# Cross attention: max scores in 13 chunks of 494 keys, one at every step behind the value products of that step; value products four slots further behind

## The reference, cut to what matters

```python
q = x @ Wq; k = ctx @ Wk; v = ctx @ Wv            # ctx: 6404 x 128
s = einsum('qd,kd->qk', q_h, k_h) / sqrt(8)       # 1024 x 6404 scores per head
p = softmax(s, axis=-1)                           # needs the max of each row
o_h = p @ v_h                                     # 1024 x 8
```

## Time and profile before

| | us |
|---|---|
| median of 3 runs (4591.18 to 4597.89) | 4594.65 |
| the profiled execution's own time | 4605.47 |
| its span | 4603.5 |
| PE busy | 3836.9 (83%) |
| DVE busy | 3455.6 (75%) |
| ACT busy | 2867.1 (62%) |
| mean granted TensorE clock, of full speed | 0.878 |

### The profile page before, as it was taken

One profiled execution on the slowest core, in us unless ns is written; L12 is line 12 of the kernel. 1 busy time (PEld: TensorE's weight loads), 2 busy tenths in 40 slices (PEclk: granted clock), 3 DMA queues, 4 the chain that ended last, 5 costly groups with the idle time before them and its releaser, 6 DMA issues. The chain is left out here.

```text
span 4603.5 us, 83947 instructions
## 1 busy us (share of the span) xinstructions
PE 3836.9 (83%) x34296; PEld 1292.0 (28%) x34358; DVE 3455.6 (75%) x3306; ACT 2867.1 (62%) x4073; POOL 258.4 (6%) x183
## 2 busy tenths in 40 slices
PE   6897489999999965899999999389838999999996
PEld 2564122222222212222222222145412222222221
DVE  4332389989989715989999895489839999998981
ACT  0332147778877841678778788245424777877884
POOL 3000100000000010000000000234310000000000
PEclk9556679999999985899999999699957999999998
DMA  2000401111111013111111100200040111011100
GB/s 87 1 0 0 85 12 25 25 25 18 20 25 25 4 32 69 24 25 17 22 25 25 23 15 4 52 13 5 3 85 12 25 25 25 15 24 25 25 4 20
DMA packets 54250, 113.98 MB, mean 25 GB/s; under 512 B 9424, under 2 KB 44368, under 8 KB 48912
## 3 DMA queue, kind: packets, MB, share of 16 engines
q1 hardware_dynamic: 53904, 109.09, 13.4%
HBM read 83.46 MB, written 25.50 MB: 24 GB/s over the span
## 5 line engine op out<-in xcount | busy, mean ns | idle before, releaser
L1537 DVE TENSOR_REDUCE chunk_max<-max_scores 128x2 f32<-128x1024 f32 (+1 forms) x2496 | 2801.3, 1179 | 325.4 <-PE max_scores L1420 304.6
L1518 ACT ACTIVATE probs<-scores 128x512 f32<-128x512 f32 (+1 forms) x3231 | 2475.9, 809 | 664.0 <-PE scores L1446 634.3
L1473 PE MATMUL values_sum<-probs,values 128*9 128x256 f32 x19584 | 1402.7, 392 | 1.7 <-ACT probs L1518 1.7
L1446 PE MATMUL scores<-queries,key_ring 49*128 49x512 bf16 x4800 | 1251.4, 392 | 80.7 <-ACT probs L1518 48.9
L1420 PE MATMUL max_scores<-key_ring,queries 48*128 48x512 bf16 (+1 forms) x4992 | 949.7, 396 | 246.5 <-DVE chunk_max L1537 195.0
L1473 PEld LDWEIGHTS values_sum<-probs,values 128*9 128x9 f32 x19584 | 383.8, 90 | 852.9 <-issue 575.3
L1446 PEld LDWEIGHTS scores<-queries,key_ring 49*128 49x128 bf16 x4800 | 309.8, 94 | 912.3 <-ACT probs L1518 762.3
L1420 PEld LDWEIGHTS max_scores<-key_ring,queries 48*128 48x128 bf16 x4992 | 245.6, 95 | 681.9 <-DVE chunk_max L1537 618.8
L1059 ACT ACTIVATE probs<-scores 128x512 f32<-128x512 f32 x256 | 138.4, 592 | 106.1 <-PE scores L1011 106.1
L1085 DVE TENSOR_REDUCE chunk_max<-max_scores 128x1024 f32 (+1 forms) x128 | 154.9, 1213 | 21.4 <-PE max_scores L967 21.3
L1548 DVE COPY values_sum_s<-values_sum 128x256 f32<-128x256 f32 x48 | 20.0, 416 | 187.7 <-PE values_sum L1473 187.7
(11 more groups left out here) (179 smaller groups left out, 2054.3 us busy)
## 6 DMA issues: line engine op xcount, KB each, us to landing
key_ring<-k_parts SPq DMA_DIRECT2D x96, 300.2 KB
key_ring<-k_parts SPq DMA_DIRECT2D x96, 200.1 KB
k_parts<-k_part SPq DMA_DIRECT2D x108, 128.0 KB, 2.3
key_ring<-k_parts SPq DMA_DIRECT2D x96, 100.1 KB
o_whole<-values_sum_s SPq DMA_DIRECT2D x48, 128.0 KB, 9.2
queries<-q_parts SPq DMA_DIRECT2D x36, 128.0 KB
context<-in_ctx_t SPq DMA_DIRECT2D x1, 3202.0 KB, 17.0
q_parts<-q_part SPq DMA_DIRECT2D x12, 256.0 KB, 2.8
```

The lines of the kernel that those rows point to most:

```text
L1446: return pe.matmul(sc[:, g % 3, :], keys(rows, h, P * t, P * (t + 1)), qb[rows, q], start=True, stop=True)
L1473: mm = pe.matmul(acc[32 * b:32 * b + WV, 0:QBLOCK], vb[rows, h, t, :], pr[rows, slot, QBLOCK * (b % 2):QBLOCK * (b % 2 + 1)], start=(t == ...
L1518: act.activation(pr[:, a % RING:a % RING + b - a, :], sc[:, a % 3:a % 3 + b - a, :], ACT.Exp)\
L1537: dve.tensor_reduce(mx[:, h % 2, c, :, j], mxb[:, w % 2, :, 0:width], AX.X, ALU.max)\
```

## The change

Three things, all in how `cross_attention` orders and cuts its work.

1. The chunks of max scores are 494 keys wide, the last 6404 - 12 x 494 = 476. There are still 13, so 52 entries per head. (`CHUNK` stays 512 elsewhere.)
2. `entries_through` counts slots at every step, so entries become due at odd steps too, and PE works them behind the value products of the step, not ahead of them.
3. `tiles_through` lets value products lag four slots more, drops the hold at the start of a head, and starts a new head's value products at the next odd step after the one that ended the last head's.

```diff
-HOLD = 6
+MAX_CHUNK = 494
+VALUE_LAG = 2
+HEAD_GAP = 2
 def entries_through(op):
-    slots = slots_through(op - op % 2)
+    slots = slots_through(op)
...
-    done, total = [], 0
+    done, total, head_end = [], 0, 0
     for op in range(NOPS):
         if op % 2 == 1 and op >= 3:
-            slots = slots_through(op - 2)
-            ready = tiles_in(slots)
-            if slots % HEAD_SLOTS < HOLD:
-                ready = min(ready, NTILE * (slots // HEAD_SLOTS))
-            total = max(total, min(ready, total + 2))
+            ready = tiles_in(max(0, slots_through(op - 2) - 2 * VALUE_LAG))
+            for _ in range(2):
+                next_head = total > 0 and total % NTILE == 0
+                if total < ready and not (next_head and op < head_end + HEAD_GAP):
+                    total += 1
+                    if total % NTILE == 0:
+                        head_end = op
         done.append(total)
...
-                width = min(CHUNK, M - CHUNK * c)
+                width = min(MAX_CHUNK, M - MAX_CHUNK * c)
...
             for n in range(NOPS):
                 score_op(n)
+                for i in range(tiles_by[n - 1] if n else 0, tiles_by[n]):
+                    values(i)
                 for w in range(entries_through(n - 1) if n else HEAD_UNITS + LEAD, entries_through(n)):
                     max_step(w)
-                for i in range(tiles_by[n - 1] if n else 0, tiles_by[n]):
-                    values(i)
```

More of the change, by code:

```diff
@@ L1420, in max_step @@
                     mm = pe.matmul(mxb[:, w % 2, half, 0:width], qb[rows, HALF * h + P * j:HALF * h + P * (j + 1)],
-                                   keys(rows, h, CHUNK * c, CHUNK * c + width), start=True, stop=True)
+                                   keys(rows, h, MAX_CHUNK * c, MAX_CHUNK * c + width), start=True, stop=True)
                 mm.then_inc(max_scores, 1)
```

## The result

The changed kernel takes 4455.6 us (median of 4 runs) against 4593.7. One of its four runs, 5548.38 us at a mean granted clock of 0.593, was a slow one and stands outside the ratio; the other three are 4443.2 to 4459.5, with 4451.8 as their median. The ratio is 0.9684, 95% interval 0.9661 to 0.9706. The forecast was 4448 us, with a range of 4375 to 4545. The profiled execution took 4451.81 us (span 4449.9).

A forecast was written before the change was run, and what follows sets the result against it. DVE was taken as the bound in the scored stretches. A head of 57.7 + 3.6 + 0.3 = 61.6 us against 64.9, over 44.7 heads, gains 147 us: 4458 profiled, 4448 as median, range 4375 to 4545.

The forecast's parts named there:

- New head: One head's time after the change: 57.7 floor, 3.6 mid-head and 0.3 border, 61.6 us against 64.9.
- signs of being wrong: Clock still at 0.97, mid-head entries every 1.18 us or more, or ACT waits growing as PE's fall.
- The 2.8 us per head: DVE's loss around the narrow last chunk, fed at the old rate; equal chunks of 494 would remove all 2.8 us.
- mid-head excess: Time per mid-head entry above DVE's floor: 0.056 us before, taken as 0.07 after, 3.6 us a head.
- my lower bound of 0.037 (the path alone): Mid-head: buffer free to reduce started takes 3.39 us for three entries, 0.037 each over DVE's 1.093.
- the old path: The same mid-head path at the old pitch: 3.43 us against 3.39, 0.013 an entry over.
- Entries one at a time: Mid-head: a pair's two entries are split by scores and value products; excess between 0.037 and 0.093 us an entry.
- The 2.0 us a head: Mean head's loss to the lowered clock, falling just behind a head's end; the change was expected to keep it up.
- rival 1: Clock still falls at head borders, PE waiting about 1.0 us for the copy; gives back 2.0 a head, 4537 us; 0.18.
- Border: New head's first tile waits for the copy; DVE runs dry by 0 to 0.5 us, taken as 0.3 a head.
- The gain of 3.3 a head: Head falling from 64.9 to 61.6 us, times 44.7 heads: 147 us gained.

The follow-up runs named there:

- the plan onto two tiles: Changed kernel with odd entries planned onto steps with two tiles, between those tiles, and the entry after the maxima's turn directly behind it: 4561.7 us, ratio 0.9930.
- the border alone: Kernel before with only the value products' changed lag and head start (`tiles_through`): 4534.0 us, ratio 0.9850.
- the hole: Changed kernel with a new head's value products begun one odd step later, leaving one pair of steps without any at each border: 4463.3 us, one run.

## Why the prediction was right, and where its terms were not

*Bound and place.* Right: the gain lies in the scored stretches, nearly all of it as DVE's idle time (254 to 113.5 us; forecast about 120), at the same number of DVE's instructions. New head 61.4 us against 61.6. None of the signs of being wrong came: the clock reads 0.99 in the stretches, mid-head is below 1.18, and waits for ACT fell.

*Width.* The 2.8 us per head of the earlier trace rows were charged to the narrow chunk. Only 52.6 / 44.7 = 1.2 of them end at its reduces. Most of the others, 46.6 us in the stretches or 1.0 a head, follow the cast of the turned maxima, a 0.28 us instruction fed at the pace of a 1.13 us one, and 37.9 us of them are still there. The mid-head excess over DVE's 1.093, taken as 0.07, is 0.041 in the piece shown and 0.044 as the mean over heads, near my lower bound of 0.037 (the path alone). That bound was itself mis-summed: it took 1.22 us for a reduce that lasts 1.18, and with 1.18 the path gives 3.35 us, 0.024 an entry; and by the same terms the old path is 3.39 us, no excess at all, and not 3.43. In my sum the narrowing took away 2.8 a head and gave back the growth of the mid-head excess; I booked it as the largest gain, and the runs show 29 us alone and nothing that can be measured on top of the order.

*Entries one at a time.* Here the reasoning failed by its sign. I let the new order cost 0.014 an entry against mid-head before and gave it no gain of its own. It is the largest part, 143 us when alone where all three parts give 155; some 58 of the 143 stand beside the clock. The excess of 0.056 in the kernel before, which the path did not explain, goes with the blocked second entry. PE in a mid-head pair with two entries, before:

```profile
1289.20 0.39 PE L1446 MATMUL scores<-queries,key_ring 49*128 49x512 bf16 x2
1289.43 0.38 PE L1420 MATMUL max_scores<-key_ring,queries 48*128 48x512 bf16 x2
1290.31 0.39 PE L1420 MATMUL max_scores<-key_ring,queries 48*128 48x512 bf16 x2 [0.51 <-DVE chunk_max L1537]
1290.54 0.38 PE L1446 MATMUL scores<-queries,key_ring 49*128 49x512 bf16 x1
```

The second entry waits for its buffer, and the single score begins 1.34 us behind the double one, where it is 0.45 in the earlier trace rows. Over the stretches it is later than 0.8 us in 483 of the 1368 pairs recorded, and in 167 of 1455 in the changed kernel. Spreading the entries, even ahead of the value products, removes this, and brings mid-head to 0.02 over its pitch at 512 keys. That the lost time went by way of ACT and the next double score is the reading that fits; no run shows it by itself. The delay isn't all that sets the rate either: in the plan onto two tiles only 38 single scores are late, and mid-head is 1.199.

*The clock.* The 2.0 us a head were somewhat large (half speed falls from 201 to 66 us, DVE's idle time beside it from 76.0 to 23.7, which is 1.2 a head; the border alone, with what it costs, gave 67 / 44.7 = 1.5). I named one change as the cure, the end of the pair without value products, where the order of the entries alone does as much. PE's wait of 1.06 us for the copy, which rival 1 feared, came as forecast in size, but on one head in three, not on each (18.5 us of waits in the whole profile), and with a fall at fewer than half of them. So what makes the clock fall at one border and not at the next is open. The Trainium skill (TensorE: Matmul & The Clock Gate, "A second HAM failure mode: psum-queue depth-cycling") has short idle times of PE between groups of products as a cause of a clock that goes up and down. By that rule the changed kernel, with its many waits, would still see it do so, and the trace agrees only in part: mid-heads with waits for DVE and ACT in many pairs run at 1.00, and the 8 falls left all stand at borders.

*Border.* Forecast 0.3 us of DVE's time a head, measured 10.5 / 44.7 = 0.23 in the two reduces behind the copy, as far as it doesn't fall in a stretch at half speed.

*Sum.* The gain of 3.3 a head was +2.8 narrow, +2.0 clock, +2.4 - 3.6 mid-head, -0.3 border. Measured it is 1.1 narrow, 1.2 clock, 1.2 mid-head and the waits ahead of the cast (0.3 of it reduces that stand closer, so that DVE's busy time shrinks), 0.2 behind the cast, and 0.2 lost at the border: 3.5. Where the gain lies and which engine bounds it was foreseen; that the number came out within 8 us was luck, since too large gains from the narrow chunk and the clock stood against a mid-head loss that did not come, and mid-head gained instead.

## What to carry to other kernels

When two engines pass work through two buffers, write down for each engine the path from "buffer free" to "next piece ready" over what stands between in its order; here the bound engine's idle time was spread evenly over mid-head, and shortening its own pieces only moved it. Look for two pieces that wait for the same buffers and stand side by side ahead of work that a third engine needs; spread them, and put them where the pair has room. A part that seems to carry the gain is known only from the run with that part alone and the run with all but it.

## What was not expected of the hardware

The granted clock fell at head borders with no long idle time of PE ahead of it: single waits of 0.69 and 0.53 us before the change, one of 1.06 after, and a head with such a fall takes 62.7 us instead of 61.3. No single wait decides it: the 1.06 us wait passed without a fall at 8 of 15 borders, that of 1.07 us at 13 of 15 with chunks of 512, and with the hole, where PE never waits for the copy, there were 11 falls. Either of two changes of order removed most of the falls. And PE's fp32 value products begin 0.31 us behind a bf16 score, where scores and entries begin 0.22 behind each other; with one tile a step PE pays that more often, which is part of why it is slower than two at every other one.
